# A three-layer decoder step on one core: the value fold's small products dealt over the four quarters of the TensorE array, and the calls up to the thirteenth expert unit put in another order

## What is computed

```python
x = x + attn(layernorm(x), w_qkv, ln_w, w_proj)            # windows of 32, 16 heads of 8, causal
# cross attention: q from x, k and v from the context
q = (xn @ w_q);  k, v = split(context @ w_kv)
attn = softmax((q * SCALE) @ k.T);  out = (attn @ v) @ w_out + b_out
x = x + out * tanh(gate)
# experts
h = einsum('td,edf->etf', x, gate_w);  u = einsum('td,edf->etf', x, up_w)
y = einsum('etf,efd->etd', silu(h) * u, down_w)
x = x + sum over chosen e of weight[t, e] * y[e, t] + shared experts
```

## Time and profile before

| what | before |
|---|---|
| median of 3 runs | 188.43 us (188.37 to 188.7) |
| time of the profiled execution | 188.91 us |
| span of the profiled execution | 187.2 us |
| PE busy | 175.6 us, 94% |
| DVE busy | 139.7 us, 75% |
| POOL busy | 120.7 us, 64% |
| ACT busy | 107.4 us, 57% |
| granted clock of TensorE | full in all 40 slices |
| the value fold's line (L1704) in the chain that ended last | 3.3% of the span |

### The profile page before, as it was taken

How to read it: one execution, slowest core, us unless ns; L and a number is a source line. 1 busy time by engine, 2 the same in 40 slices (tenths; PEclk the granted TensorE clock), 3 DMA queues, 4 the chain that set the end, 5 groups by cost and what they waited for, 6 DMA issues and landing times.

```text
span 187.2 us, 4577 instructions
## 1 busy us (share of the span) xinstructions
PE 175.6 (94%) x1685; PEld 133.3 (71%) x1685; DVE 139.7 (75%) x308; ACT 107.4 (57%) x211; POOL 120.7 (64%) x178
## 2 busy tenths in 40 slices
PE   5999999999899989998999999999999999999992
PEld 5798776667666657778778675766677888888881
DVE  5767595868968987899989869982277667775665
ACT  6378768667666553564595394344255666555540
POOL 4473899815465786966555502038999999998700
PEclk9999999999999999999999999999999999999999
DMA  5977510000001000220000002719976554400003
GB/s 141 268 240 207 157 33 5 2 4 4 4 2 29 0 18 14 57 69 4 2 0 0 4 2 79 208 50 278 364 219 175 164 160 157 127 7 0 2 0 112
DMA packets 17718, 15.75 MB, mean 84 GB/s; under 512 B 2224, under 2 KB 13568, under 8 KB 17568
## 3 DMA queue, kind: packets, MB, share of 16 engines
q1 hardware_dynamic: 16832, 15.13, 27.6%
q10 hardware_dynamic: 864, 0.33, 0.6%
HBM read 14.86 MB, written 0.59 MB: 83 GB/s over the span
## 4 chain that ended last, share of the span: by engine, by line
PE 74%; DVE 12%; POOL 6%; issue 4%; ACT 3%; DVEq 0%; POOLq 0%; ACTq 0%
PE banks L1718 6%; PE banks L1783 5%; PE banks L1744 5%; PE banks L1765 5%; PE banks L1767 4%; PE banks L1766 4%; PE banks L1768 4%; PE banks L1770 4%; PE banks L1769 4%; PE banks L1704 3%; PE banks L1675 3%; PE banks L1787 3%; PE banks L1788 3%; PE banks L1786 3%; PE banks L1689 2%
## 5 line engine op out<-in xcount | busy, mean ns | idle before, releaser
L865 ACT ACTIVATE s<-banks 128x512 f32<-128x512 f32 x36 | 21.4, 599 | 31.1 <-PE banks L1767 31.0
L526 POOL TENSOR_TENSOR act<-act,vbd 128x512 f32<-128x512 f32 x14 | 22.2, 1586 | 1.9 <-DVE act L1324 0.8
L715 POOL TENSOR_TENSOR gu_lo<-gu_w,gu_hi 128x256 fp32r<-128x256 f32 x14 | 11.2, 800 | 16.4 <-ACT gu_hi L871 16.4
L1324 DVE TENSOR_TENSOR act<-s,banks 128x512 f32<-128x512 f32 x20 | 13.7, 685 | 10.2 <-ACT s L865 8.8
L526 POOL TENSOR_TENSOR qk_fold<-qk_fold,vbd 128x512 f32<-128x512 f32 x12 | 19.2, 1607 | 0.8 <-DVE qk_fold L1324 0.4
L1324 DVE TENSOR_TENSOR qk_fold<-s,banks 128x512 f32<-128x512 f32 x16 | 10.9, 686 | 9.9 <-PE banks L1770 6.7
L1765 PE MATMUL banks<-x3hi,gu_lo 128*128 128x512 f32 x36 | 17.7, 490 | 0.2 <-POOL gu_lo L715 0.2
L1744 PE MATMUL banks<-vo_fold,p2T 128*128 128x128 f32 x128 | 16.6, 279 | 1.2 <-ACT p2T L859 1.1
L535 POOL TENSOR_SCALAR ve<-mv 128x1 f32<-128x1 f32 x16 | 3.2, 197 | 22.0 <-DVE mv L1106 21.8
L1744 PEld LDWEIGHTS banks<-vo_fold,p2T 128*128 128x128 f32 x128 | 15.3, 192 | 2.6 <-ACT p2T L859 2.0
L518 POOL TENSOR_TENSOR kbd<-kbd,rs 128x1024 f32<-128x1024 f32 x8 | 15.2, 1902 | 2.4 <-DVE rs L1208 2.3
(11 more groups left out here) (177 smaller groups left out, 467.5 us busy)
## 6 DMA issues: line engine op xcount, KB each, us to landing
vbd<-comb_rows SPq DMA_DIRECT2D x30, 256.0 KB, 3.7
wkv_sb<-in_L_xattn_w_kv_dram SPq DMA_DIRECT2D x1, 1024.0 KB, 8.2
gu_w<-in_L_ffn_gate_w_dram SPq DMA_DIRECT2D x16, 64.0 KB, 2.2
gu_w<-in_L_ffn_up_w_dram SPq DMA_DIRECT2D x16, 64.0 KB, 3.3
vo_fold<-in_L_ffn_down_w_dram SPq DMA_DIRECT2D x1, 960.0 KB, 6.5
wq_sb<-in_L_xattn_w_q_dram SPq DMA_DIRECT2D x1, 512.0 KB, 6.2
wout_sb<-in_L_xattn_w_out_dram SPq DMA_DIRECT2D x1, 512.0 KB, 6.5
x<-in_x_dram SPq DMA_DIRECT2D x3, 128.0 KB, 2.9
```

Source lines behind the costliest of these rows:

```text
L526: engine.tensor_tensor(act_of(k), act_of(k), spread[:, j % SPREAD, :], ALU.mult).then_inc(scale_early if j < RING else scale_s, 1)
L865: sc.activation(sil[:, k % 2, :], bank[2 * (k % 2)], ACT.Silu).then_inc(sil_s, 1)
L1324: dve.tensor_tensor(act_of(k), sil[:, k % 2, :], bank[2 * (k % 2) + 1], ALU.mult).then_inc(g_s, 1)
```

## The change

Two things. In `fold(("VW", j))` both waits come ahead of the first product, and the loops are turned: the 16 products go over the four quarters (row half, column half) in turn, (0,0), (1,1), (0,1), (1,0), where before eight products in a row used one row half. The products themselves, their operands and their places are the same.

```diff
-                    for h in range(2):
-                        if h == 0:
-                            pe.wait_ge(half_s, NPAIR // 2 + j)
-                        else:
-                            pe.wait_ge(f_copied, copies_before(u, {FOLD + h}))
-                        hs = slice(DH * h, DH * (h + 1))
-                        for b in range(B):
-                            bs = slice(b * CTX, (b + 1) * CTX)
-                            for pair, c in ((2 * j, h), (2 * j + 1, 1 - h)):
+                    pe.wait_ge(half_s, NPAIR // 2 + j)
+                    pe.wait_ge(f_copied, copies_before(u, {FOLD + 1}))
+                    for b in range(B):
+                        bs = slice(b * CTX, (b + 1) * CTX)
+                        for swap in range(2):
+                            for h in range(2):
+                                hs = slice(DH * h, DH * (h + 1))
+                                pair, c = (2 * j + 1, 1 - h) if swap else (2 * j, h)
                                 last = pe.matmul(bank[FOLD + h][CTX * c:CTX * (c + 1), b * D:(b + 1) * D],
                                                  kv_sb[hs, pair, 1, bs], wout_sb[hs, pair, :], start=True, stop=True)
```

And the lists of all engines but the sync queue are put in another order up to about unit 12. No call is added or dropped. A few lines stand for the many:

```diff
 (PE, layer 1)
             fold(("A", 0))
+            scores1(2)
             values1(0)
             fold(("kv", 4))
+            scores1(3)
             transpose_y(0)
-            scores1(2)
             transpose_p1(1)
+            fold(("kv", 5))
             project_out(0)
-            fold(("kv", 5))
...
 (DVE, routing)
             softmax2_sum(7)
-            split_x3(4)
             multiply(0)
+            multiply(1)
             group_scores(early)
             residual2(6)
...
             multiply(7)
+            scale_act(dve, 0)
             expert_weights(late)
-            scale_act(dve, 0)
             multiply(8)
...
 (PE, routing)
-            transpose_combine(1)
             down(2)
+            transpose_combine(1)
             gate_up(10)
```

More of the change, by code:

```diff
@@ L1394, in _ @@
             norm_stats(1, 6)
+            norm_y(7)
             softmax2_sum(0)
-            norm_y(7)
             softmax2_max(1)
@@ L1437, in _ @@
             norm_stats(2, 7)
-            multiply(1)
+            split_x3(5)
+            choose_experts(early)
+            multiply(2)
             split_x3(6)
-            choose_experts(early)
             split_x3(7)
-            multiply(2)
             expert_weights(early)
@@ L1471, in _ @@
             multiply(7)
+            scale_act(dve, 0)
             expert_weights(late)
[L1473 removed]
             multiply(8)
+            multiply(9)
             scale_act(dve, 1)
[L1476 removed]
+            multiply(10)
             scale_act(dve, 2)
[L1478 removed]
             scale_act(dve, 3)
@@ L1851, in _ @@
             project_v(3)
+            scores1(1)
             fold(("kv", 2))
-            scores1(1)
             fold(("kv", 3))
@@ L1873, in _ @@
             transpose_y(2)
+            scores1(5)
             transpose_p1(3)
-            scores1(4)
             project_out(2)
             fold(("kv", 7))
-            scores1(5)
             values1(3)
@@ L1881, in _ @@
             transpose_y(3)
+            scores1(6)
             transpose_p1(4)
+            project_out(3)
             fold(("VW", 0))
-            project_out(3)
-            scores1(6)
             values1(4)
+            scores1(7)
             transpose_p1(5)
             transpose_y(4)
-            scores1(7)
+            fold(("x2", 0))
             project_out(4)
-            fold(("x2", 0))
             values1(5)
             fold(("VW", 1))
+            transpose_y(5)
             transpose_p1(6)
-            transpose_y(5)
             scores2(0)
@@ L1901, in _ @@
             transpose_y(6)
-            transpose_p1(7)
+            scores2(1)
             project_out(6)
-            scores2(1)
+            values1(7)
             fold(("x2", 2))
-            values1(7)
+            transpose_y(7)
             fold(("VW", 3))
-            transpose_y(7)
             scores2(2)
@@ L1922, in _ @@
             transpose_p2(2)
+            logits(0)
             scores2(5)
-            logits(0)
+            transpose_xn3(1)
             output2(2, 0)
-            transpose_xn3(1)
             output2(2, 1)
+            logits(1)
             transpose_p2(3)
             scores2(6)
-            logits(1)
+            output2(3, 0)
             transpose_xn3(2)
-            output2(3, 0)
             output2(3, 1)
+            transpose_p2(4)
+            scores2(7)
+            output2(4, 0)
             logits(2)
-            transpose_p2(4)
-            output2(4, 0)
+            transpose_xn3(3)
             output2(4, 1)
-            transpose_xn3(3)
-            scores2(7)
             logits(3)
+            gate_up(0)
             transpose_p2(5)
-            gate_up(0)
             transpose_xn3(4)
             output2(5, 0)
-            logits(4)
             output2(5, 1)
@@ L1948, in _ @@
             transpose_p2(6)
+            logits(4)
+            transpose_xn3(5)
             output2(6, 0)
-            transpose_xn3(5)
             output2(6, 1)
@@ L1957, in _ @@
             down(0)
+            gate_up(2)
             logits(6)
-            gate_up(2)
             transpose_xn3(7)
+            down(1)
             logits(7)
-            down(1)
             gate_up(3)
@@ L1972, in _ @@
             gate_up(9)
+            down(2)
             transpose_combine(1)
-            down(2)
             gate_up(10)
```

91 lines of the change are left out of this document (46 added, 45 removed).

## The result

| | before | after |
|---|---|---|
| median of 8 runs each | 188.74 us (188.37 to 189.28) | 187.94 us (187.63 to 188.29) |
| ratio, with its 95% interval | | 0.9957 (0.9945 to 0.9969) |
| profiled execution (span) | 188.91 us (187.2) | 188.09 us (186.4) |
| PE busy | 175.6 us | 172.9 us |

The change is faster by 0.8 us, a third of the forecast 2.4 us, and outside the range. Of the 1.9 us between the forecast 186.0 and 187.94, 0.3 is the starting point: the kernel before has a median of 188.74 over eight runs, where the forecast started from 188.43, the median of three. From the value fold on, lines have a number lower by one after the change (L1704 is L1703, L1786 is L1785).

A forecast was written before the change was run, and what follows sets the result against it. PE was taken to bound the kernel (94% busy), with DVE sharing the pace before the expert units. Terms -2.2 - 0.4 - 0.2 + 0.4 = -2.4 us, from 188.43 to 186.0 us; range 184.9 to 187.6.

The forecast's parts named there:

- value fold, four calls: In the four `VW` calls on PE: products dealt over four quarters take 0.97 to 1.0 us against 1.52, 2.2 us won.
- new order, 20 to 68 us: Up to layer 2's softmax: PE waits of 1.2 us gone, 0.8 us new, 0.4 us won; bounds -2.0 and +0.8.
- new order, 68 to 116 us: Layer 2 and the routing: `scores2(7)` covers ACT's copy, `group_scores` clears POOL's `norm_p2(7)`; 0.2 us won, bounds 1.1 won, 0.6 lost.
- first expert units: Late routing weights are turned behind `down(2)`, POOL starts up to 0.86 us later, `down(12)` waits: +0.4 us, bounds 0 and 0.9.
- rival in which quarters don't run four at a time: In the value fold, weight loads wait for their row half's products: 1.88 us a call, 189.6 us in all; chance 7%.
- DVE gives it back: Rival: the value fold shrinks but DVE sets the pace and PE waits elsewhere; half of 2.4 us stays, 187.2 us; 22%.
- joint wait of 0.3 us: At the fourth `VW` call: both waits ahead of the first product, only `transpose_y(7)` as cover, charged 0.3 us.
- a wait of PE at L1786's place behind POOL's first `scale_act`: Sign at the first expert units: PE would wait there, behind POOL's first `scale_act`; the forecast charged 0.4 us for the step.

## Why the forecast was wrong, step by step

| step | forecast | measured | by |
|---|---|---|---|
| value fold, four calls | -2.2 | -2.0 | length of the calls: 1.58, 1.52, 1.52, 1.52 to 1.03 or 1.04 us each |
| new order, 20 to 68 us | -0.4 | -0.3 | what is left: order kept up to 65 us only, -2.3, less the fold |
| new order, 68 to 116 us | -0.2 | +0.3 | 186.85 - 186.54, at the limit of the noise |
| first expert units | +0.4 | +1.1 | 187.94 - 186.85 |
| sum | -2.4 | -0.9 | the medians say -0.8 |

The second row is what the others leave, so that the sum closes by itself and proves nothing. With the 1.7 us that the medians give the fold (next paragraph), it would be -0.6.

**The value fold was right.** "0.97 to 1.0 us" a call came out as 1.03 to 1.04. The working that rested on the earlier trace rows carried: four quarters work at a time, and each quarter's eight records go one behind the other. A record takes 1.03 / 32 = 0.032 us where it took 0.0475. The rival in which quarters don't run four at a time has fallen. Not all of the 2.0 us reaches the end: the changed kernel differs from the run with the order alone only in the fold's loops, and the medians are 1.7 us apart (189.67 and 187.94). The fourth call is no longer in the chain that ended last, which goes over DVE there (start us, us, what):

```profile
54.24 1.03 PE banks L1703 x32
...
59.06 1.14 DVE sum L1204
...
62.81 0.30 DVE x L1187
```

So the rival *DVE gives it back* holds for a few microseconds, between the third call and `fold(x2, 3)`. It isn't what made the forecast fail: with only the two late calls put back, and DVE as busy in that stretch (11.0 of 12 us from 54 to 66, against 10.8 after the change), the time is 186.85 us.

**The step that failed is the one at the first expert units.** I worked out that POOL starts "up to 0.86 later", and charged 0.4, the middle between 0 and 0.9. Nothing in the rows spoke for the lower half. In the kernel before, PE did not wait at `down(12)`, but its operand's last step ended at 136.94, 0.06 us ahead of PE's 137.00, and POOL had been waiting for the transfer itself at 127.51. A chain without slack passes on every delay: PE and this chain were two equally long paths. The profiles put the delay of `transpose_combine(1)` at 0.85 us (120.63 - 119.30, less the offset of 0.48), the upper bound. `down(2)` ahead of it takes just that long (119.77 to 120.63). The DVE call does not come on top. It delays the weights by 0.60 us (`combine` ends at 120.24 instead of 119.16, less the offset), but they are there 0.39 us ahead of PE; the later of the two sets the time. It is still needed, since `down(2)` can't stand there without it, and by itself it costs 0.6 us. The medians put the whole at 1.1 us, and what remains between 0.85 and 1.1 isn't explained. The lowest times of the two kernels, 187.63 and 186.75, are 0.9 apart, so that part of it may be the idle time at L1572, which not all executions have.

**The order to 68 us came out near its size, by other terms.** I gave a joint wait of 0.3 us to the fourth call. In the old order it costs 1.3 to 1.5 us, at three of four calls, and in the new one some 0.15 us at the fourth. Of PE's waits, those of the `A` folds fell from 0.6 to 0.3, while the one at `values1` grew from 0.5 to 1.4 us, of which I had forecast 0.5 at the last call; it is 0.48 there (the wait at 57.95), and two more of 0.47 stand at earlier calls, where before there were two of 0.26.

**The order to 116 us most likely has the wrong sign.** `scores2(7)` did cover the copy it was moved ahead of: L1744's 1.1 us behind ACT's copies is not in the list of this stretch any more. But `multiply(1)` now stands "0.6 us in the way of `residual2(6)`", and `output2(7)` waits 0.7 us for that residual; the `xn3` transposes wait 0.9 for POOL. The 1.05 us that I hoped to win at `group_scores` mostly moved to another operation. "DVE has 1.25 us left" was the sentence to follow: the rest of a full engine is soon spent.

The sign tests of the forecast did their work: `transpose_xn3(7)` was to be 2.5 to 2.8 us earlier and was 1.6, and "a wait of PE at L1786's place behind POOL's first `scale_act`" is what took the most.

## What to carry to other kernels

- Ahead of crediting a saved piece to the end of the program, look for the second chain that meets the first later: an operand that is ready within a tenth of a microsecond of its use means two critical paths. Anything that delays the shorter-looking one is to be charged in full. Where calls on two engines are put ahead of it (here one on DVE and one on PE), the later of the two sets the delay, and a call that needs the other's result brings it along.
- Small products like these are best dealt so that a product's neighbours in the list go to other parts of the array; a wait for two banks in place of one has to be given cover by the order around it. Such a pair of edits has no separate worth: the loops alone were worth -0.4 us, and -1.7 us (189.67 to 187.94) with the order to cover them.

## What the runs showed of the hardware

In the value fold the order in which products go over the quarters decides how many run at a time. Within one quarter a record of 128 float32 columns follows the one ahead at 0.109 us, about the rate of a product on the whole array (0.111). A quarter at a time, the call is 2.29 us from first to last start and not 31 x 0.109 = 3.4, since the next quarter's records start when three of the eight of the last one are still to come. With a row half at a time two quarters are fed, and the next half starts likewise before the last one is through, which makes 1.32 us; dealt over four it is 0.84.

Row halves need not alternate from product to product: in pairs the call takes the same 0.84 us. The Trainium skill (TensorE: Matmul & The Clock Gate, The mechanism) says that a weight load overlaps running products only when the row group differs. The run in pairs does not agree: half of its products follow one of the same row half. In all four orders the starts fit that what counts is whether the next product's quarter is free. Records of L1703 that touch two stretches of 0.28 us in the run in pairs, once the call is under way:

```profile
44.90:45.18 0.28, 0.28 (x12) 0.28 (x16) 1.00 0.00 0
45.20:45.48 0.28, 0.28 (x20) 0.28 (x16) 1.00 0.00 0
```

The 20 records in a stretch, against 10 with one row half and 16 at the border of both the earlier trace rows, are the four quarters at work.
